# Local attention layers: which engine reads a projection first, and where VectorE's side steps stand

## The reference

```
x = attn_layer(shift_tokens(x), Wqkv, q_scale, k_scale, Wo) + x
x = ffn_layer(shift_tokens(x), ln_g, ln_b, W1, b1, W2, b2) + x

attn_layer: q, k, v = split(x @ Wqkv)             # 16 heads of 64
            q = l2norm(q) * q_scale; k = l2norm(k) * k_scale
            q = q*cos*scale + rotate_half(q)*sin*scale;  k likewise with 1/scale
            out = softmax over a window (32 own keys and 32 before) @ v;  return out @ Wo
ffn_layer:  xn = layernorm(x) * g + b
            a, gate = split(xn @ W1 + b1);  return a * gelu(gate) @ W2 + b2
```

## Time and profile before

| What | us |
|---|---|
| median of three runs | 6164.31 |
| the profiled execution | 6159.82 |
| its span | 6157.8 |
| PE busy, whole span | 5227.7 (85%) |
| DVE busy | 4071.6 (66%) |
| ACT busy | 2844.8 (46%) |
| POOL busy | 2347.6 (38%) |

### The profile page before, as it was taken

How to read it: one execution, slowest core, us unless ns; L and a number is a source line. 1 busy time by engine, 2 the same in 40 slices (tenths; PEclk the granted TensorE clock), 3 DMA queues, 4 the chain that set the end, 5 groups by cost and what they waited for, 6 DMA issues and landing times. The chain is left out here.

```text
span 6157.8 us, 174461 instructions
## 1 busy us (share of the span) xinstructions
PE 5227.7 (85%) x73680; PEld 3362.4 (55%) x73680; DVE 4071.6 (66%) x6338; ACT 2844.8 (46%) x5037; POOL 2347.6 (38%) x2148
## 2 busy tenths in 40 slices
PE   5878778786868778999999999999999999999997
PEld 3857667585848564444444444444444444444444
DVE  6565665566565647767777777777777777776774
ACT  4232232414132315555555555555555555555554
POOL 2232222222222315444444444444444444444441
PEclk8888888788878879999999999999999999999999
DMA  0000000000000002222222222222222222222222
GB/s 20 3 2 4 1 4 1 4 1 4 1 4 1 3 28 62 57 59 71 68 60 60 62 68 58 58 65 69 65 60 66 69 62 56 56 72 62 59 59 57
DMA packets 255860, 252.25 MB, mean 41 GB/s; under 512 B 29680, under 2 KB 248816, under 8 KB 254704
## 3 DMA queue, kind: packets, MB, share of 16 engines
q1 hardware_dynamic: 255088, 241.09, 15.6%
HBM read 29.71 MB, written 4.19 MB: 6 GB/s over the span
## 5 line engine op out<-in xcount | busy, mean ns | idle before, releaser
L1366 POOL TENSOR_TENSOR turn<-prod 128x512 f32<-128x512 f32 x768 | 983.6, 1281 | 2068.8 <-DVE prod L1406 1849.0
L1406 DVE TENSOR_TENSOR prod<-banks,tabs 128x1024 f32<-128x1024 f32 x768 | 936.9, 1220 | 638.7 <-ACT sq L1251 638.7
L1103 PE MATMUL banks<-w2s,xs 128*128 128x512 f32 x2304 | 1190.0, 599 | 38.2 <-DVE xs L1438 30.2
L1375 POOL TENSOR_TENSOR turn<-turn,rs 128x512 f32<-128x512 f32 x768 | 784.9, 1043 | 6.1
L661 POOL TENSOR_TENSOR ao<-at,msk 128x512 f32<-128x512 f32 x288 | 388.0, 1358 | 1045.6 <-PE banks L413 564.2
L1137 PEld LDWEIGHTS banks<-msk,turn 128*128 128x128 f32 x3072 | 354.1, 141 | 550.1 <-issue 469.8
L1137 PE MATMUL banks<-msk,turn 128*128 128x128 f32 x3072 | 473.2, 277 | 65.6 <-ACT kx L1281 63.1
L1417 DVE TENSOR_REDUCE ss<-sq 128x8 f32<-128x512 f32 x768 | 519.1, 676 | 0.0
L615 ACT ACTIVATE p<-banks 128x512 f32<-128x512 f32 x288 | 172.0, 597 | 722.1 <-PE banks L413 722.1
L855 DVE TENSOR_TENSOR tr<-tr,banks 128x512 f32<-128x512 f32 x240 | 165.3, 689 | 510.1 <-PE banks L437 508.8
L1251 ACT ACTIVATE sq<-banks 128x512 f32<-128x512 f32 x768 | 454.9, 592 | 66.4 <-PE banks L1103 66.3
(11 more groups left out here) (202 smaller groups left out, 9901.4 us busy)
## 6 DMA issues: line engine op xcount, KB each, us to landing
v<-v_tok SPq DMA_DIRECT2D x1152, 132.0 KB
v<-v_tok SPq DMA_DIRECT2D x384, 66.0 KB
v<-v SPq DMA_DIRECT2D x188, 132.0 KB, 2.4
w2s<-in_weights SPq DMA_DIRECT2D x10, 768.0 KB, 4.7
tabs<-in_rot SPq DMA_DIRECT2D x40, 128.0 KB, 2.8
w2s<-in_weights SPq DMA_DIRECT2D x1, 2713.5 KB, 10.9
w2s<-in_weights SPq DMA_DIRECT2D x10, 256.0 KB, 3.8
xin<-in_x SPq DMA_DIRECT2D x8, 256.0 KB, 2.8
```

Source lines behind the costliest of these rows:

```text
L1103: pe.matmul(a_bank(use), xs[:, t % 2, b * P:(b + 1) * P], w[:, at:at + 512], start=True, stop=True).then_inc(a_done, 1)
L1366: gp.tensor_tensor(turn[:, r % ROTS, :, :].rearrange(halves, s=2), prod[:, r % 2, 0, :, :].rearrange(halves, s=2), prod[:, r % 2, 1, :, :] ...
L1375: gp.tensor_tensor(turn[:, r % ROTS, :, :], turn[:, r % ROTS, :, :], along(rs[:, q % 2, b, :], DH), ALU.mult).then_inc(rot_done, 1)
L1406: v.tensor_tensor(prod[:, r % 2, :, :, :], a_bank(use).rearrange("p (h d) -> p h d", h=HU).unsqueeze(1) .to_broadcast([P, 2, HU, DH]), tab ...
```

## The change

Three things change, all in `local_layers`.

- Projections 0 and 1 are read by VectorE first: `rotate` waits for the product alone, and `square` waits for the release by `rotate`. A product into that bank then waits for the square as well, and `sums` waits for the square.
- VectorE's order in a step becomes: kept keys (where due), scores, rotate 0, rotate 1, normalise, sums 0, sums 1, then the feed-forward steps. Steps 0 and 4 of the feed-forward move from in front of `normalise` to the end; `shifted_in` moves from g % 8 == 7 to g % 8 == 5.
- ScalarE's order becomes: first turned heads, exponential, (at g % 8 == 5 the Gelu table), second turned heads, square 0, turned exponents, square 1, values, and the rest as before.

```
                     def bank_free(n):
                         if n >= 2:
                             pe.wait_ge(a_free[n % 2], n // 2)
+                            if n - 2 in sq_use:
+                                pe.wait_ge(sq_done, sq_use[n - 2] + 1)
 ...
                     def square(g, n):
-                        a.wait_ge(a_done, use + 1)
                         if i < 8:
                             r = U * 8 + i
+                            a.wait_ge(a_free[use % 2], use // 2 + 1)
 ...
                         if attend:
                             exponents(g)
-                        if feed:
-                            square(g, 0)
+                        if 8 <= g and g % 8 == 5:
+                            a.preload_act_table_set(GELU)
                         if order:
                             take_heads(order[1])
                         if feed:
-                            square(g, 1)
-                        if 8 <= g and g % 8 == 5:
-                            a.preload_act_table_set(GELU)
+                            square(g, 0)
                         if attend:
                             take_probs(g)
                         if feed:
+                            square(g, 1)
                             square(g, 2)
 ...
                     def rotate(g, n):
-                        v.wait_ge(sq_done, r + 1)
+                        v.wait_ge(a_done, use + 1)
                     def sums(g, n):
+                        v.wait_ge(sq_done, r + 1)
 ...
+                        if g % 4 == 0 and 2 <= U < UNITS:
+                            keep_keys(U)
                         if attend:
                             shifted_scores(g)
-                        if g % 4 == 0 and 2 <= U < UNITS:
-                            keep_keys(U)
                         if feed:
                             rotate(g, 0)
-                            sums(g, 0)
-                        if 8 <= g and g % 8 in (1, 4):
-                            ffn(g // 8 - 1, 0 if g % 8 == 1 else 4)
+                            rotate(g, 1)
                         if 0 <= g - 1 < NIT:
                             normalise(g - 1)
                         if feed:
-                            rotate(g, 1)
+                            sums(g, 0)
                             sums(g, 1)
-                        if 8 <= g and g % 8 in (1, 2, 6, 7):
+                        if 8 <= g and g % 8 == 1:
+                            ffn(g // 8 - 1, 0)
+                        if 8 <= g and g % 8 in (1, 2, 4, 6, 7):
                             ffn(g // 8 - 1, g % 8)
-                        if g % 8 == 7 and g // 8 + 2 < TILES:
+                        if g % 8 == 5 and g // 8 + 2 < TILES:
                             shifted_in(g // 8 + 2)
```

More of the change, by code:

```diff
@@ L996, in item_use @@
             return a_use["x", 4 * U - LEAD + i - 8, 2]
+        sq_use = {item_use(U, i): U * 8 + i for U in range(UNITS) for i in range(8)}
         def a_bank(n):
@@ L1253, in square @@
                             b = i - 8
+                            a.wait_ge(a_done, use + 1)
                             W = U - 2 if b < 2 else U - 1
```

## The result

The changed kernel takes 5776.29 us (median of four runs, 5771.59 to 5781.55) against 6162.0 us of the kernel before on the same chip: a ratio of 0.9374, 95% interval 0.9358 to 0.939. The direction was right, the size was not.

A forecast was written before the change was run, and what follows sets the result against it. TensorE (PE) was taken to set the time, so only its idle gaps could be won: 0.96 + 1.51 + 0.28 + 1.38 + 2.06 + 0.19 - 0.3 = 6.1 us per tile, 280 us in 46 tiles, giving 5884 us; range 5815 to 6010.

The forecast's parts named there:

- that leaves PE idle ... and only these gaps can be won: All eight steps: step length less PE's busy time leaves 7.73 of 79.4 us idle, all that can be won.
- Rival 4: Whole tile: all of PE's gaps close, 7.73 us in each of 46 tiles, 356 us, giving 5808 us; chance 0.1.
- the carry's price: Step g % 8 = 2: carry at its median 0.87 us holds the output projection 1.26 us; 0.28 us still won.
- price of the late division: Every step: division ends 0.05 us later, taken as 0.04 per step, 0.3 us per tile lost.
- if it had to sit out a whole GpSimd instruction: Carry at g % 8 = 2: waiting for a GpSimd instruction of 1.47 us would hold PE 1.85 us.
- the output projection for the residual: At g % 8 = 2: projection waits for the residual to free its bank, about 1.3 us once per tile.
- the turn of the exponents behind the table load: At g % 8 = 5: the turn starts at 13.2 instead of 12.94 us, 0.26 us lost.
- rival 3: Squares in every step come late and PE waits; at 1 us per step 92 us slower, 6256 us; chance 0.05.
- rival 1: Gain about half: 0.25 us per step for the late division, dearer steps 2 and 5; about 6022 us; chance 0.2.
- Rival 2: Work moved behind the sums delays the next maximum equally, the exponents' turn waits instead; about 6164 us; chance 0.05.

The follow-up runs named there:

- experiment 1: Changed kernel with VectorE's side steps back at their old places, only the order of reads and ScalarE's order new: 5972.24 us, 0.9689 of the kernel before.
- experiment 7: Changed kernel with only the kept keys back behind the scores at g % 8 = 0 and 4: 5811.69 us, 0.9429 of the kernel before.
- experiment 5: Changed kernel with only feed-forward step 0 (carry and residual) back in front of the division at g % 8 = 1: 5780.17 us, 0.9378 of the kernel before.
- experiment 6: Changed kernel with only feed-forward step 4 (two scalings) back in front of the division at g % 8 = 4: 5900.59 us, 0.9571 of the kernel before.

## Why the prediction was wrong

**The failed step: "that leaves PE idle ... and only these gaps can be won".** PE's busy time in a step was taken as its floor, 8.56 us for a step with one product and 71.7 for a tile. It is 8.35 and 70.0. A wait lengthens the busy time around it: the end of the turn and the start of the product overlap only when the product is not held (experiment 1). Rival 4, in which all gaps close, was priced with the same floor, at 5808; the measured time is below it, although 1.0 us of idle time a tile is left. In sum, per tile, forecast and measured (change of the mean length of the step):

| g % 8 | forecast won | measured | what differed |
|---|---|---|---|
| 0 | 0.96 | 1.10 | 0.06 hidden at a turn (experiment 7: 0.32 shown, 0.38 lost); 0.06 is the first tile's step alone, 11.22 us before |
| 1 | 1.51 | 1.50 | equal by chance: 1.41 idle in the mean, 0.08 hidden; see below for the cause |
| 2 | 0.28 | 0.89 | floor 0.21; the carry's price |
| 3, 6, 7 | 1.38 | 2.02 | 0.2 hidden at each of three products |
| 4 | 2.06 | 2.24 | hidden at two waits |
| 5 | 0.19 | 0.53 | 0.25 hidden (PE busy 10.57 to 10.32); 0.10 from the three tiles of the kernel before with a half-clock slice |
| price of the late division | -0.3 | 0 | the handover shrank from 0.10 to 0.06 |

The measured column adds up to 8.3 us, 381 us in 46 tiles; the forecast to 6.1. The tile of the earlier trace rows is not typical at g % 8 = 5: its step lasts 11.28 us with 0.70 idle, where the medians are 11.01 and 0.45.

**The carry.** Its price of 0.87 was taken from the median of the old place. At the new place it had two values:

```profile
L1473 DVE COPY y<-y x42: 159/161/1280, 2499.1 to 5736.3; 128x4 f32<-128x4 f32 x42
```

34 of 42 took 0.16 us and 8 about 1.3. Step 2 lasts 9.00 us in most tiles and 10.1 in eight. Both ends were in the text ("if it had to sit out a whole GpSimd instruction"); the middle one, which was chosen, does not occur there. In one of the cheap tiles the residual frees the bank and the projection follows:

```profile
4274.02 0.16 DVE L1473 COPY y<-y 128x4 f32<-128x4 f32 x1
...
4274.28 0.69 DVE L1483 TENSOR_TENSOR y<-banks,y 128x512 f32<-128x512 f32 x1
...
4275.12 1.10 PE L1189 MATMUL banks<-ot,w2s 128*128 128x512 f32 x2 [0.49 <-DVE y L1483]
```

**What was right, and what only came out.** The new waits stand where they were put: the output projection for the residual (0.79 a tile in the mean, 1.26 forecast) and the turn of the exponents behind the table load (11.2 us in 45 tiles, 0.25 each, 0.26 forecast). In the step shown with the result the squares end 0.7 and 0.1 us before the products that need their banks start, and no product waits for one, so rival 3 failed. The division ends 0.05 later and costs nothing, so rival 1's bound of 0.25 per step is far off. Rival 2, the handing on of a wait, is true of step 2 alone: experiment 5 shows that the move of feed-forward step 0 wins nothing. The prediction booked 1.51 and 0.28 to the moves there; the reads alone bring steps 1 and 2 to 8.34 and 8.35 (experiment 1), together what they take in the changed kernel. So the 1.51 of step 1 has the wrong cause, and that its number was met is luck. The 161.6 us of waits for the division were also misread: they are three waits a tile and not two, at g % 8 = 1, 2 and 4 (1.41, 0.31 and 1.77 us in the mean).

## What to carry to other kernels

Here the idle time that the profile showed in front of a held product was less than what the wait cost, 0.46 against 0.67 us: look at the start-to-start time of the same pair of instructions where nothing is held, and take that as the floor. A step that is moved off one wait should be followed to the next consumer of what it frees; here the residual's bank made the move of one step worthless until the step was put into an idle gap. The small VectorE instructions that met GpSimd here had two or more separate prices and not a mean; ask which one the new place meets.

## What the runs showed of the hardware

A wait of 1.9 us of PE in every tile went with 26 slices of 3.4 us at half the granted clock (experiment 6), and with 22 in experiment 1, where the same wait stood in the same step. The kernel before has 2.06 us of idle time in that step, 1.77 of it in front of the same turn, and 3 such slices in the same stretch; the changed kernel has none. Why the kernel before was spared was not settled; the price of a stall can thus be more than its length.

VectorE's two-input instructions in SBUF were slow or fast by the neighbour: the table scaling (L1469), 0.56 us before, takes 1.52 to 1.54 in all 40 cases at its new place, and the first scaling (L1497) 0.68 instead of 1.39. The first scaling began while a GpSimd instruction ran in 46 of 48 cases before, and in none now.

```profile
L1469 DVE TENSOR_TENSOR tabs<-tabs,w2s x40: 1519/1529/1542, 2444.7 to 5211.2; 128x256 f32<-128x256 f32 x40
L1497 DVE TENSOR_TENSOR xc<-xc,msk x48: 679/680/691, 2453.1 to 5748.1; 128x512 f32<-128x512 f32 x48
```
